# Three hops of a graph network: two iterations a step, rows scaled in place

## The reference, cut to what matters

```python
for l in range(N_LAYERS):
    ...
    mask = jnp.clip(jax.nn.sigmoid(log_alpha) * (ZETA - GAMMA) + GAMMA, 0.0, 1.0)
    rowsum = jax.ops.segment_sum(mask, row, num_segments=n) + 1e-06
    d_inv_sqrt = jnp.clip(rowsum ** (-0.5), 0.0, 10.0)
    vals = mask * d_inv_sqrt[row] * d_inv_sqrt[col]
    x = jax.ops.segment_sum(vals[:, None] * x[col], row, num_segments=n)
    out = out + x
```

## Time and profile before

| | us |
|---|---|
| median of 3 runs | 11239.33 |
| their lowest and highest | 11235.35, 11245.48 |
| span of the profiled execution, first to last instruction | 11234.0 |
| the first hop, first gather to the end of L3010 | 7027.31 to 7461.60 |

### The profile page before, as it was taken

The page is one execution under the profiler, slowest core; times in us unless marked ns, Lnnn a source line. Parts: engine busy times, 40 slices in busy tenths (PEclk is TensorE's granted clock), DMA queues, the critical chain, the costliest instruction groups (busy, mean ns, idle before and its releaser), DMA issues. The chain is left out here.

```text
span 11234.0 us, 448798 instructions
## 1 busy us (share of the span) xinstructions
PE 8366.9 (74%) x151748; PEld 7090.9 (63%) x151749; DVE 8649.2 (77%) x21890; ACT 6257.6 (56%) x14808; POOL 5047.9 (45%) x5196
## 2 busy tenths in 40 slices
PE   6444444378889997996877788778887788777877
PEld 6444344278877777886756667467675576655855
DVE  6776667578889999998686785976868858679367
ACT  0222222169987777997405536975359863589410
POOL 1777777734430001111371471753726627356057
PEclk8555555589999998998999989999889998899999
DMA  6655553269989997996996998979989789897997
GB/s 220 185 179 183 180 168 90 70 215 330 331 281 259 258 248 261 322 322 210 329 328 247 290 271 301 312 248 288 272 285 316 242 302 272 274 322 256 373 326 264
DMA packets 1297726, 2929.45 MB, mean 261 GB/s; under 512 B 381368, under 2 KB 925682, under 8 KB 1272400
## 3 DMA queue, kind: packets, MB, share of 16 engines
q1 hardware_dynamic: 956540, 1976.18, 51.0%
q0 software_dynamic: 296704, 823.09, 24.7%
q10 hardware_dynamic: 44116, 125.96, 4.0%
HBM read 1753.54 MB, written 1104.99 MB: 254 GB/s over the span
## 5 line engine op out<-in xcount | busy, mean ns | idle before, releaser
L574 POOL DMA_INDIRECT rows_s<-place_rec,place_index x1568 | 1523.3, 971 | 531.0 <-issue 514.2
L665 PE MATMUL place_slot_ps<-place_runs,place_oh_turned 50*128 50x100 f32 x3136 | 728.5, 423 | 1072.5 <-ACT place_oh_turned L613 1025.6
L2959 POOL DMA_INDIRECT hop_x<-cols_all,hop_index x864 | 988.3, 1144 | 1024.1 <-ACT hop_index L2968 757.5
L665 PEld LDWEIGHTS place_slot_ps<-place_runs,place_oh_turned 50*128 50x128 f32 x3136 | 683.1, 327 | 1103.3 <-issue 1091.3
L2977 ACT ACTIVATE hop_parts<-hop_x,mask 128x64 f32<-128x64 f32 x5184 | 1258.7, 336 | 10.7 <-issue 6.6
L3024 PEld LDWEIGHTS hop_sums_ps<-hop_parts,hop_onehot 128*128 128x128 bf16 x18144 | 587.4, 97 | 650.6 <-issue 649.9
L1853 POOL DMA_DIRECT2D cm_onehot<-hot_d x288 | 152.7, 531 | 1774.4 <-POOLq L107 977.8
L3024 PE MATMUL hop_sums_ps<-hop_parts,hop_onehot 128*128 128x64 bf16 x18144 | 687.7, 193 | 334.2 <-DVE hop_parts L3006 321.5
L2764 POOL DMA_INDIRECT mask_cols<-cols_all,mask_index x432 | 432.6, 1001 | 790.9 <-ACT mask_index L2788 679.6
L2761 POOL DMA_INDIRECT mask_cols<-cols_all,mask_index x432 | 672.1, 1556 | 254.0 <-ACT mask_index L2788 162.7
L622 ACT COPY place_rec<-keys 128x32 f32 (+1 forms) x98 | 21.5, 219 | 1309.7 <-DMA place_rec<-in_e 1261.1
(11 more groups left out here) (498 smaller groups left out, 28533.6 us busy)
## 6 DMA issues: line engine op xcount, KB each, us to landing
cols_all<-att_in_rows SPq DMA_DIRECT2D x216, 896.0 KB
mask_onehot<-hot_s SPq DMA_DIRECT2D x108, 1792.0 KB
cols_all<-hop_in_rows SPq DMA_DIRECT2D x216, 896.0 KB
hop_onehot<-hot_s SPq DMA_DIRECT2D x864, 224.0 KB
rows_all<-blank SPq DMA_DIRECT2D x72, 1808.0 KB
ct_u<-rows_all SPq DMA_DIRECT2D x288, 452.0 KB
cm_v<-rows_all SPq DMA_DIRECT2D x288, 448.0 KB
cm_onehot<-hot_d POOLq DMA_DIRECT2D x288, 448.0 KB
```

The costliest lines, as they stand in the source:

```text
L574: nc.gpsimd.indirect_dma_start(m.rows_s.rearrange("p n w -> (p n) w"), bass.IndirectOffsetOnAxis(index[:, j, t:t + 1], 0), rec[:, j, t, :] ...
L665: last = nc.tensor.matmul(slot_ps[b][:, t, 0:2 * NBK], oh_turned[:, b, t, :], runs[:, b, t, :], start=True, stop=True)
L2959: nc.gpsimd.indirect_dma_start(x[:, n, :, :].rearrange("p c f -> p (c f)"), None, table, bass.IndirectOffsetOnAxis(index[:, n:n + 1], 0)). ...
```

## The change

A step now handles two iterations, a pair. The loops still run over iterations, but most waits and signals stand only at the even or the odd one.

- `onehot` has six places of two iterations; SP issues one load for two iterations (3584 bytes a partition).
- ScalarE scales five tiles of each iteration (`OWN`), and writes the result over the gathered rows in `x`; it waits for the gather alone. VectorE scales the other two tiles of both iterations in one instruction of 256 elements a partition (`scale_rest`), also in place, which waits for both gathers.
- The two subtractions cover both iterations, 896 elements. `parts` keeps two of the three parts, in three places for pairs; `summed` counts pairs, and is set 3 ahead, by VectorE.
- TensorE does the same matmuls, waits once for a pair and signals once; GpSimd waits at even iterations.

```diff
-        onehot = sb("onehot", [P, 3, 4, BATCH, P], bf16)
+        onehot = sb("onehot", [P, PAIR_SLOTS, 2, BATCH, P], bf16)
...
-        parts = sb("parts", [P, 4, 3, BATCH * F])
+        parts = sb("parts", [P, 3, 2, 2 * BATCH * F])
...
-                    sp.dma_start(as_words(onehot[:, s, i, :, :]), m.hot_s[:, bass.ds(it, 1), :]).then_inc(came[s * 4 + i], 16)
+                def load(it, slot):
+                    sp.dma_start(onehot[:, slot, :, :, :].rearrange("p i t n -> p (i t n)").bitcast(fp32).rearrange("p (b w) -> p b w", b=2),
+                                 m.hot_s[:, bass.ds(it, 2), :]).then_inc(came[slot], 16)
...
-                    if look_ahead(it, 12):
-                        sp.wait_ge(summed, it + 5)
-                        load(it + 12, s, i)
+                    if i % 2 == 0 and look_ahead(it, 12):
+                        sp.wait_ge(summed, k * 6 + s * 2 + i // 2 + 4)
+                        load(it + 12, s * 2 + i // 2)
...
-                    if not isinstance(it, int) or it > 11:
-                        pool.wait_ge(summed, it - 5)
+                    if i % 2 == 0 and (not isinstance(it, int) or it > 11):
+                        pool.wait_ge(summed, k * 6 + n // 2 - 1)
...
-                    act.wait_ge(arrived[s * 4 + i], k * 16 + 16)
-                    act.wait_ge(summed, it + 1)
+                    n = s * 4 + i
+                    act.wait_ge(arrived[n], k * 16 + 16)
...
-                    for t in range(BATCH - 1):
-                        last = nc.scalar.activation(parts[:, i, 0, t * F:(t + 1) * F], x[:, s * 4 + i, t, :], ACT.Copy,
-                                                    scale=mask[:, bass.ds(it * BATCH + t, 1)])
-                    last.then_inc(weighted, 1)
-                act.sem_inc(summed, 4)
+                    for t in range(OWN):
+                        final = nc.scalar.activation(x[:, n, t, :], x[:, n, t, :], ACT.Copy, scale=mask[:, bass.ds(it * BATCH + t, 1)])
+                    final.then_inc(weighted, 1)
...
-                def scale_seventh(it, n, k):
+                def scale_rest(it, n, k):
                     dve.wait_ge(arrived[n], k * 16 + 16)
-                    dve.wait_ge(summed, it + 1)
+                    dve.wait_ge(arrived[n + 1], k * 16 + 16)
                     dve.sem_inc(gate, 1)
-                    nc.vector.tensor_tensor(parts[:, n % 4, 0, (BATCH - 1) * F:], x[:, n, BATCH - 1, :],
-                                            mask[:, bass.ds(it * BATCH + BATCH - 1, 1)].to_broadcast([P, F]),
-                                            ALU.mult).then_inc(seventh, 1)
+                    there = x[:, n:n + 2, OWN:BATCH, :]
+                    by = mask[:, bass.ds(it * BATCH, 2 * BATCH)].rearrange("p (i t) -> p i t", i=2)[:, :, OWN:BATCH]
+                    nc.vector.tensor_tensor(there, there, by.unsqueeze(3).to_broadcast([P, 2, BATCH - OWN, F]), ALU.mult).then_inc(scaled, 1)
...
+                    if i % 2:
+                        return
+                    n = s * 4 + i
+                    pair, slot = k * 6 + n // 2, n // 2 % 3
+                    whole = rows[:, n:n + 2, :].rearrange("p i w -> p (i w)")
+                    rest, lowest = parts[:, slot, 0, :], parts[:, slot, 1, :]
+                    dve.wait_ge(weighted, it + 2)
+                    dve.wait_ge(scaled, pair + 1)
+                    dve.wait_ge(summed, pair + 1)
                     dve.sem_inc(gate, 1)
                     nc.vector.tensor_tensor(rest, whole, upper(whole), ALU.subtract).then_inc(halved, 1)
-                    if more:
-                        n = s * 4 + i + 1
-                        scale_seventh(it + 1, n % 12, k + n // 12)
-                    dve.wait_ge(halved, it + 1)
+                    if look_ahead(it, 2):
+                        scale_rest(it + 2, (n + 2) % 12, k + (n + 2) // 12)
+                    dve.wait_ge(halved, pair + 1)
                     dve.sem_inc(gate, 1)
-                    nc.vector.tensor_tensor(last, rest, upper(rest), ALU.subtract).then_inc(parted, 1)
+                    nc.vector.tensor_tensor(lowest, rest, upper(rest), ALU.subtract).then_inc(parted, 1)
...
-                    pe.wait_ge(came[s * 4 + i], k * 16 + 16)
-                    pe.wait_ge(parted, it + 1)
+                    n = s * 4 + i
+                    pair, slot = k * 6 + n // 2, n // 2 % 3
+                    if i % 2 == 0:
+                        pe.wait_ge(came[n // 2], k * 16 + 16)
+                        pe.wait_ge(parted, pair + 1)
...
-                    last.then_inc(summed, 1)
+                    if i % 2:
+                        final.then_inc(summed, 1)
```

More of the change, by code:

```diff
@@ L2915, in stage_hop @@
 def stage_hop(nc, m, name, mask, inv_root, acc, last):
+    OWN = 5
+    PAIR_SLOTS = 6
     ctx = Stage(nc)
@@ L2925, in sb @@
             return ctx.enter_context(nc.sbuf_tensor(f"{name}_{n}", s, d))
-        onehot = sb("onehot", [P, 3, 4, BATCH, P], bf16)
+        onehot = sb("onehot", [P, PAIR_SLOTS, 2, BATCH, P], bf16)
         x = sb("x", [P, 12, BATCH, F])
         index = sb("index", [P, 12], i32)
-        parts = sb("parts", [P, 4, 3, BATCH * F])
+        parts = sb("parts", [P, 3, 2, 2 * BATCH * F])
         sums = ctx.enter_context(nc.psum_tensor(f"{name}_sums_ps", [P, 56, F], fp32))
         warm = ctx.enter_context(nc.psum_tensor(f"{name}_warm_ps", [P, 512], fp32))
-        came, arrived = [sem(f"came{n}") for n in range(12)], [sem(f"arrived{n}") for n in range(12)]
-        indexed, weighted, seventh, halved, parted, summed, gate = (sem(n) for n in (
-            "indexed", "weighted", "seventh", "halved", "parted", "summed", "gate"))
+        came, arrived = [sem(f"came{n}") for n in range(PAIR_SLOTS)], [sem(f"arrived{n}") for n in range(12)]
+        indexed, weighted, scaled, halved, parted, summed, gate = (sem(n) for n in (
+            "indexed", "weighted", "scaled", "halved", "parted", "summed", "gate"))
         table = m.cols_all.rearrange("p n w -> (p n) w")
+        rows = x[:].rearrange("p n c f -> p n (c f)")
         with nc.Block() as block:
@@ L2938, in _ @@
             def _(sp):
-                def load(it, s, i):
-                    sp.dma_start(as_words(onehot[:, s, i, :, :]), m.hot_s[:, bass.ds(it, 1), :]).then_inc(came[s * 4 + i], 16)
+                def load(it, slot):
+                    sp.dma_start(onehot[:, slot, :, :, :].rearrange("p i t n -> p (i t n)").bitcast(fp32).rearrange("p (b w) -> p b w", b=2),
+                                 m.hot_s[:, bass.ds(it, 2), :]).then_inc(came[slot], 16)
                 def step(it, s, i, k, more, _):
-                    if look_ahead(it, 12):
-                        sp.wait_ge(summed, it + 5)
-                        load(it + 12, s, i)
-                for n in range(12):
-                    load(n, n // 4, n % 4)
+                    if i % 2 == 0 and look_ahead(it, 12):
+                        sp.wait_ge(summed, k * 6 + s * 2 + i // 2 + 4)
+                        load(it + 12, s * 2 + i // 2)
+                for n in range(PAIR_SLOTS):
+                    load(n * 2, n)
                 each12(sp, step)
@@ L2955, in step @@
                         pool.wait_ge(indexed, k * 3 + s + 1)
-                    if not isinstance(it, int) or it > 11:
-                        pool.wait_ge(summed, it - 5)
+                    if i % 2 == 0 and (not isinstance(it, int) or it > 11):
+                        pool.wait_ge(summed, k * 6 + n // 2 - 1)
                     pool.sem_inc(gate, 1)
-                    nc.gpsimd.indirect_dma_start(x[:, n, :, :].rearrange("p c f -> p (c f)"), None, table,
+                    nc.gpsimd.indirect_dma_start(rows[:, n, :], None, table,
                                                  bass.IndirectOffsetOnAxis(index[:, n:n + 1], 0)).then_inc(arrived[n], 16)
@@ L3017, in step @@
                 def step(it, s, i, k, more, _):
-                    pe.wait_ge(came[s * 4 + i], k * 16 + 16)
-                    pe.wait_ge(parted, it + 1)
+                    n = s * 4 + i
[3 more added lines that the diff above has]
+                        pe.wait_ge(parted, pair + 1)
                     blocks = blocks_s.of(it, i)
                     pe.sem_inc(gate, 1)
+                    at = i % 2 * BATCH * F
                     for t in range(BATCH):
-                        for q in range(3):
-                            last = nc.tensor.matmul(block_of(sums, blocks[0]), onehot[:, s, i, t, :],
-                                                    upper(parts[:, i, q, t * F:(t + 1) * F]), start=False, stop=False)
-                    last.then_inc(summed, 1)
+                        for value in (x[:, n, t, :], parts[:, slot, 0, at + t * F:at + (t + 1) * F],
+                                      parts[:, slot, 1, at + t * F:at + (t + 1) * F]):
+                            final = nc.tensor.matmul(block_of(sums, blocks[0]), onehot[:, n // 2, i % 2, t, :],
```

(3 more changed lines are left out.)

8 lines of the change are left out of this document (3 added, 5 removed).

## The result

The changed kernel takes 11319.84 us (median of 4 runs, 11312.54 to 11322.32) against 11240.46 us for the kernel before (11235.35 to 11245.48): the ratio is 1.0071, 95% interval 1.0058 to 1.0083. It is slower by 79 us, where 11347 us and a loss of 108 us were forecast. The profiled execution's span is 11319.7 us against 11234.0. From the start of a hop's first gather to the start of its last VectorE instruction (L3018, formerly L3010) the three hops take 450.0, 454.0 and 467.6 us where they took 430.9, 431.2 and 437.2. That is 72 of the 86 us between the two spans. The other 13 lie outside the hops, where the change does nothing and where the profiled executions of this document's kernels differ by as much (all before, between and after the hops together: 9919 to 9949 us).

A forecast was written before the change was run, and what follows sets the result against it. ScalarE sets today's 1.455 us an iteration; GpSimd's gathers, held by VectorE, would become the bound at 1.57. 11234 + 99 + 9 = 11342 us profiled, the runs' median 5 above: 11347 us, range 11200 to 11460.

The forecast's parts named there:

- the sentence on the lead: GpSimd's gathers: waiting for pair p-5 gives the same lead as waiting for iteration n-10 did; no cost was added.
- rival C: Hops much slower, 11546 us: hold locks at 1.80 an iteration, or the five-pair loop gets too long; chance 0.09.
- Prices of instructions: VectorE in the hops: a subtraction over 896 elements takes 1.09 us, the scaling of two tiles for two iterations 0.42.
- ScalarE at 1.215 an iteration, under 80 of 100 us: ScalarE in the hops: five ACTIVATEs instead of six, minus 0.24 us an iteration if alone; its window falls from 100.
- GpSimd becomes the bound, c = 1.57: Hop gathers: 1.255 us undisturbed plus the hold by VectorE, between 1.51 and 1.63 an iteration; +99 us over 864 iterations.
- its own last sign: Hop gathers: if they stay at 0.95 to 1.15 us, the forecast is wrong and the hold is the failed place.
- rival A: Gathers at L2959: the hold doesn't grow in the loop, so the kernel is faster, 11157 or 11200 us; chance 0.15.
- The hold grows with the instruction: GpSimd's gathers wait for a running VectorE subtraction's end; longer ones hold longer, single gathers near 1.8 to 1.9 us.
- Fill and drain 3 us a hop: Start and end of each hop: filling and draining in pairs costs 3 us a hop, +9 (between 0 and 15).
- TensorE's holes cost nothing: TensorE in the hops: same matmuls, now in pairs of 2.2 us with holes between, costed at nothing.
- Loads: SP's one-hot loads, half as many and twice as large: price nothing; were DMA the limit, SAGE's pace of 1.40.
- VectorE 2.45 a pair: VectorE in the hops: two subtractions and one scaling take 1.01 + 0.43 + 1.01 us, 1.23 an iteration.
- likeliest case: The hops: the forecast's own outcome, 1.51 to 1.70 us an iteration, 11295 to 11460 us; chance 0.68.

The follow-up runs named there:

- Experiment 6: The kernel before, the gather of iteration n waiting for iteration n-9 instead of n-10: 1.0001, 11249 us against 11245.
- experiment 2: The changed kernel, the gather of pair p waiting for pair p-6 instead of p-5: 0.9991 of the kernel before, 11226 us against 11236.
- experiment 9: The changed kernel, scaling of the next pair moved behind the second subtraction, wait for pair p-5 kept: 1.0013 of the kernel before, 11252 us against 11241.
- 1: The changed kernel, each subtraction issued as two instructions of 448 elements: 1.0088 of the kernel before, 11329 us against 11236.
- experiment 3: The changed kernel with two more unread warming matmuls on TensorE after each pair: 1.0059 of the kernel before, 11299 us against 11236.
- experiment 8: The kernel before with only the loads of the one-hots paired, six places of two iterations: 1.0000, 11242 us against 11245.
- experiment 7: The kernel before, iterations one at a time, rows scaled in place, five tiles by ScalarE and two by VectorE: 0.9905, 11137 us against 11245.
- 11: The unpaired kernel with rows scaled in place, gathers waiting for iteration n-12 instead of n-10: 0.9896 of the kernel before, 11129 us against 11241.
- 12: The changed kernel with scaling behind the second subtraction, wait for pair p-6, and subtractions split into 448 elements: 1.0029 of the kernel before, 11268 us against 11240.

## Why the forecast's number was right and its reason wrong

**The failing step** is the sentence on the lead: the gather of pair p waits for pair p-5, "That is the same lead in whole pairs", and with it the sum under rival C, 11.7 us in a ring "closed over five pairs", of 15.7 us that are there; so the wait for TensorE stood in the sum at nothing. It forgot the order on VectorE. The second subtraction of pair q-1 stands behind the scaling of pair q, which waits for the rows of both iterations of q. So the ring is: gather of pair q, landing, scaling of q, second subtraction of q-1, TensorE on q-1, gather of pair q+4. It closes over four pairs, eight iterations. The forecast's own 11.7 us over eight iterations are 1.46 each, before any hold. The kernel before has this order too, but closes over nine iterations and carries one iteration's work in it instead of two. Experiment 6 shows that eight would do there, so it should be the pair's longer way round, more than the count, that makes the ring bind; no run separates the two.

The ring is to be seen in the changed kernel's second hop. GpSimd first; counted from the hop's first gather, 8829.27 is number 216, the second of its pair, and 8840.71 number 223, the first gather four pairs later:

```profile
8829.27 0.94 POOL L2963 DMA_INDIRECT hop_x<-cols_all,hop_index  x1 [1.65 <-issue]
...
8840.71 0.99 POOL L2963 DMA_INDIRECT hop_x<-cols_all,hop_index  x1 [2.39 <-PE hop_sums_ps L3037]
```

VectorE and TensorE between them:

```profile
8834.82 0.43 DVE L2995 TENSOR_TENSOR hop_x<-hop_x,mask 128x256 f32<-128x256 f32 x1 [4.32 <-DMA hop_x<-cols_all,hop_index]
8835.16 1.08 DVE L3013 TENSOR_TENSOR hop_parts<-hop_parts 128x896 f32<-128x896 f32 x1
```

```profile
8836.92 0.23 PE L3037 MATMUL hop_sums_ps<-hop_x,hop_onehot 128*128 128x64 bf16 x1 [5.16 <-DVE hop_parts L3013]
```

Gather at 8829.27, scaling when its rows are there at 8834.82, subtraction of the pair before to 8836.24, TensorE from 8836.92 after 5.16 us without work, then the gather that waited 2.39 us for it. All three engines stood still in turn. This is a bad case: over the 91 pairs of the three hops whose gather had to wait, the same way takes 10.5, 10.6 and 10.9 us on average, and here 11.44. A hole of 1.65 us that the profile gives no reason for stands ahead of it, and TensorE is at the lower of its two levels from 8836.23 to 8839.65 (the window 8800 to 8850 grants 0.91 on average).

With the 1.4 to 1.6 us between the pair's own two gathers, these rings take 11.95, 12.20 and 12.44 us on average in the three hops, where GpSimd alone would come round in 8 x (1.138 + 0.30) = 11.5. So it waits. Over eight iterations they are 1.49, 1.52 and 1.56 us each, and the gathers of the three hops lie 1.53, 1.54 and 1.56 apart; the 0.03 us left in the first hop isn't accounted for. Opening the ring at either end, by the lead (experiment 2) or by the order (9), takes away 90 and 65 us; shortening the instructions (1) takes away none, since what a shorter hold gives back in the ring, the split's longer second subtraction (about 0.07 us) may take again. That last reason is argued, not shown.

Point by point:

- *Prices of instructions*: right (1.09, 0.42).
- *ScalarE at 1.215 an iteration, under 80 of 100 us*: the price was right, the share is 85.95. The pace of 1.53 for 1.57 explains 2 points of that (1.215 / 1.53 = 79). The rest is that busy time isn't spacing: five ACTIVATEs start 0.239 apart, but the last one's 0.334 counts in full when no other follows at once, so a burst is busy for 1.30 us, and 1.30 / 1.53 is 85 of 100.
- *GpSimd becomes the bound, c = 1.57*: wrong in this kernel. The mean gather was forecast at 1.27 and measures 1.138. The sum lets every request that meets an instruction wait for its end and VectorE never idle; here 168 of 864 requests meet an instruction that has just begun and go free, and 252 meet none. By its own last sign ("wrong if the gathers stay at 0.95 to 1.15") the forecast failed, and its rival A should have come, at 11157 to 11200 us; the time went the other way, because neither had the ring.
- *The hold grows with the instruction*: right (0.915 for 0.925); it makes up a gather's 0.19 us over 0.945, as it made up 0.20 before, and so isn't the cause of the loss.
- *Fill and drain 3 us a hop*: not there. Besides the pace of the gathers, the hops differ by what follows the last gather's start, and that is 1.5, 0.5 and 1.5 us shorter than before.
- *TensorE's holes cost nothing*: wrong, since TensorE's turn is part of the ring. What the lower clock adds in them is small (experiment 3: 70 us less of it go with 14 us) and isn't measured apart.
- *Loads*: right (experiment 8). The SAGE stage's 1.40 isn't the limit of the DMA engines either: experiment 7 runs at 1.33.
- *VectorE 2.45 a pair*: a small slip, the scaling stands there with 0.43 and further down with its spacing of 0.34; nothing hangs on it.
- *Range and signs*: measured 11320, inside 11200 to 11460, and inside the likeliest case's 11295 to 11460.

The number came out by luck: two errors of about one size met. The hold was put at 0.12 us an iteration too much, and the ring, 0.09 of waiting in the first hop and more in the third, at nothing.

The best version that the runs found is the one that leaves the pairs out: scaling in place, five tiles and two, iterations one at a time (experiment 7, 0.9905, or 11, 0.9896).

## What to carry to other kernels

Before changing the grain of a pipeline, write down the ring that limits it (transfer, landing, each engine's place in its own order, release) and count over how many steps it closes; an instruction that waits for the next step's data takes one step away, and with coarser steps that one is larger. Idle time of a busy in-order engine may be a symptom of such a ring, and a mean duration calibrated in a stage without the ring says nothing about it. When a change has two halves, time each alone: here one half is worth 107 us and the other costs 187.

## What the runs showed of the hardware

- GpSimd's indirect DMA is held by a VectorE tensor_tensor with both operands in SBUF that is already running when it starts (by 0.024 to 0.045 us at least) and still runs 0.125 us later, to that instruction's end: 0.915 us beside one of 1.09, 2.33 beside one of 3.42. One that begins with the gather or just after it holds nothing, though it runs for 1.0 us more. Plain DMAs from the same queue aren't (536 to 601 ns over 864 issues). The Trainium skill, page "SBUF — State Buffer", section "Who interferes with whom", has the rule for GpSimd instructions that read SBUF; the holds here agree with it, if it is the read of the indices that waits.
- The hold locks GpSimd's phase to VectorE's. With VectorE's round at 1.31 us it locks at 0.06 a gather (experiment 7), at 2.98 for a pair at 0.06 and 0.42 (12), so it can cost less on a fuller VectorE (99.33 of 100 us in experiment 7) than on an emptier one (84.23 in the changed kernel, 0.19 a gather).
- A VectorE instruction that needs the result of the one just ahead starts 0.15 to 0.18 us after its end, where an independent one starts 0.08 before it: two such waits a pair cost 0.23 + 0.26 = 0.49 us (experiment 9).
